# A searched order of steps for the third and the last attention of a four-layer transformer kernel

## What is computed

```python
x = x + tanh(g_xattn[2]) * L2_xattn(layernorm(x), ctx)   # 16 heads of 16, 154 context rows, softmax
x = x + tanh(g_ffn[2]) * L2_ffn(layernorm(x))            # 8 experts, two per token
x = x + tanh(g_xattn[3]) * L3_xattn(layernorm(x), ctx)   # 16 heads, queries and keys scaled to length 1,
                                                         # layernorm of (query + output) with gain and shift
x = x + tanh(g_ffn[3]) * L3_ffn(layernorm(x))            # 16 routed experts, two per token, and a shared one
```

## Time and profile before

| | us |
|---|---|
| median of three runs | 1379.36 |
| lowest and highest of them | 1375.1, 1379.63 |
| the profiled execution | 1367.15 |
| its span, first to last instruction | 1365.4 |
| PE busy in it | 1221.3 |
| DVE, ACT, POOL busy in it | 683.4, 473.6, 284.0 |
| third attention and its routing | 557 to 778 of the span |
| last attention and its routing | 942 to 1131 of the span |

### The profile page before, as it was taken

How to read it: one execution, slowest core, us unless ns; L and a number is a source line. 1 busy time by engine, 2 the same in 40 slices (tenths; PEclk the granted TensorE clock), 3 DMA queues, 4 the chain that set the end, 5 groups by cost and what they waited for, 6 DMA issues and landing times.

```text
span 1365.4 us, 19716 instructions
## 1 busy us (share of the span) xinstructions
PE 1221.3 (89%) x7073; PEld 765.9 (56%) x7073; DVE 683.4 (50%) x1969; ACT 473.6 (35%) x903; POOL 284.0 (21%) x372
## 2 busy tenths in 40 slices
PE   4999979999999765799999799993899988999997
PEld 2545444345667624445555599992455555666664
DVE  5565454577545485666566522224546771222114
ACT  1154524443232173124443133331665312223220
POOL 4200020020200102121024422222322361222220
PEclk9799989999999987679999699997999998999998
DMA  9994010001000100000002777755000224444415
GB/s 249 273 273 141 1 58 1 0 1 62 1 1 1 35 0 0 2 20 2 1 31 94 243 218 210 215 167 167 1 1 5 99 83 132 148 154 154 145 61 185
DMA packets 106494, 124.06 MB, mean 91 GB/s; under 512 B 15554, under 2 KB 90942, under 8 KB 106398
## 3 DMA queue, kind: packets, MB, share of 16 engines
q1 hardware_dynamic: 99406, 103.92, 26.3%
q0 software_dynamic: 6992, 18.88, 3.7%
HBM read 73.92 MB, written 48.86 MB: 90 GB/s over the span
## 4 chain that ended last, share of the span: by engine, by line
PE 81%; DVE 7%; issue 4%; ACT 3%; POOL 3%; DMA 1%; SPq 1%; DVEq 0%; POOLq 0%; ACTq 0%
PE bank L1225 9%; PE bank L848 6%; PE bank L1259 5%; PE bank L774 5%; PE bank L1301 5%; PE bank L1268 5%; PE bank L868 5%; PE bank L909 4%; PE bank L1059 3%; PE bank L912 3%; PE bank L757 3%; PE bank L715 2%; PE bank L1016 2%; PE bank L921 2%; POOL x_slots L1768 2%
## 5 line engine op out<-in xcount | busy, mean ns | idle before, releaser
L1225 PE MATMUL bank<-scratch 128*128 128x320 f32 (+3 forms) x480 | 151.2, 472 | 0.6 <-issue 0.6
L2098 DVE TENSOR_REDUCE scratch<-bank 128x2 f32<-128x308 f32 x256 | 103.9, 472 | 62.1 <-PE bank L848 61.7
L1372 ACT ACTIVATE scratch<-bank 128x512 f32<-128x512 f32 x192 | 99.2, 604 | 64.9 <-PE bank L875 48.1
L1225 PEld LDWEIGHTS bank<-scratch 128*128 128x128 f32 (+1 forms) x480 | 86.1, 183 | 60.2 <-issue 28.5
L2606 DVE TENSOR_TENSOR scratch<-scratch,bank 128x320 f32<-128x320 f32 (+3 forms) x60 | 31.4, 525 | 170.3 <-PE bank L1225 170.1
L1741 POOL TENSOR_SCALAR rstd<-mv 128x4 f32<-128x4 f32 x36 | 9.0, 249 | 475.5 <-DVE mv L1879 461.9
L848 PE MATMUL bank<-scratch 32*128 32x308 f32 x512 | 80.5, 512 | 3.8 <-DVE scratch L2098 1.7
L1259 PEld LDWEIGHTS bank<-scratch 128*128 128x128 f32 x624 | 77.3, 195 | 2.6 <-issue 0.7
L2589 DVE TENSOR_TENSOR scratch<-bank,weights 128x512 f32<-128x512 f32 x39 | 27.0, 692 | 102.8 <-PE bank L1259 102.8
L1863 POOL DMA_INDIRECT y_back<-scratch x48 | 45.2, 941 | 157.6 <-ACT scratch L1609 138.4
L1259 PE MATMUL bank<-scratch 128*128 128x128 f32 x624 | 77.6, 279 | 0.3 <-issue 0.3
(11 more groups left out here) (385 smaller groups left out, 2223.6 us busy)
## 6 DMA issues: line engine op xcount, KB each, us to landing
scratch<-in_L_ffn_W SPq DMA_DIRECT2D x47, 512.0 KB, 4.0
x_slots<-zeros SPq DMA_DIRECT2D x1, 17680.0 KB, 76.4
scratch<-y_back SPq DMA_DIRECT2D x16, 512.0 KB, 7.8
scratch<-in_L_ffn_w_gate SPq DMA_DIRECT2D x16, 352.0 KB, 3.1
scratch<-in_L_ffn_w_up SPq DMA_DIRECT2D x16, 352.0 KB, 3.8
x_slots<-zeros SPq DMA_DIRECT2D x1, 5200.0 KB, 94.2
scratch<-x_slots SPq DMA_DIRECT2D x39, 130.0 KB, 3.0
y_back<-zeros SPq DMA_DIRECT2D x1, 4352.0 KB, 39.9
```

The lines of the kernel that those rows point to most:

```text
L1225: last = pe.matmul(bk[0:fn, 0:n], w[s][:, k, m * P:m * P + fn], moving(k), start=k == 0, stop=k == DK - 1)
L1372: act.activation(v["PT"][:, n % 2, j, :], bk[:], ACT.Exp, scale=float(v["hd"]) ** -0.5).then_inc(RP.read, 1)
L2098: dve.tensor_reduce(v["mx"][:, TPC * c + t, r, 2 * m:2 * m + 2], bk[:, 0:2 * M].rearrange("p (e k) -> p e k", k=M), AX.X, ALU.max)\
```

## The change

The tables `FIRST`, `EACH` and `LAST` get a new order for the third attention (`2`) and the last one (`3`). The entries of the first attention (`0`) and the hand-written list of the second stay. Since a row falls away in the table, every later line number is lower by one. On DVE, one wait for the engine's own earlier writes is put ahead of `down` of the shared expert, because `res`, which writes the same rows of X, may now stand directly before it. The diff, cut to two lines of a table and the code:

```diff
             3: [
-                ("combine", 0), ("stats", 0), ("normal", 0), ("yT", 0), ("combine", 1), ("stats", 1), ("proj", 0),
-                ("normal", 1), ("unit", 0), ("turn", 0)]}
+                ("combine", 0), ("stats", 0), ("normal", 0), ("combine", 1), ("yT", 0), ("proj", 0), ("stats", 1),
+                ("unit", 0), ("turn", 0), ("normal", 1)]}
...
                 elif what == "down":
+                    st.wait()
                     expert_out(p, E3, c, lambda t: gate)
```

More of the change, by code:

```diff
@@ L633, in build @@
             2: [
-                ("stats", 3), ("scores", 0, 0), ("norm", -1, 2), ("av", -1, 3), ("normal", 2), ("max", 1, 0, 0),
-                ("rem", 0), ("next b2", -3), ("max", 1, 0, 1), ("next scatter", -3), ("next yT", -2), ("av", 0, 0),
-                ("max", 1, 1, 0), ("scores", 0, 1), ("max", 1, 1, 1), ("norm", -1, 3), ("yT", 2), ("next lg", -2),
-                ("max", 1, 2, 0), ("turn back", -1), ("max", 1, 2, 1), ("av", 0, 1), ("max", 1, 3, 0),
-                ("scores", 0, 2), ("max", 1, 3, 1), ("next top", -2), ("proj", 2), ("tail", -1), ("next gates", -2),
@@ L639, in build @@
[L639 to L647 removed]
+                ("normal", 2), ("scores", 0, 0), ("max", 1, 0, 1), ("next b2", -3), ("yT", 2), ("next yT", -2),
@@ new lines, in build @@
+                ("max", 1, 1, 0), ("rem", 0), ("max", 1, 1, 1), ("norm", -1, 2), ("norm", -1, 3), ("scores", 0, 1),
+                ("max", 1, 2, 0), ("proj", 2), ("next lg", -2), ("stats", 3), ("turn back", -1), ("max", 1, 2, 1),
+                ("av", 0, 0), ("max", 1, 3, 0), ("scores", 0, 2), ("max", 1, 3, 1), ("next top", -2), ("av", 0, 1),
+                ("max", 2, 0, 0), ("tail", -1), ("next scatter", -3), ("next gates", -2), ("next stats", -1),
+                ("scores", 0, 3), ("norm", 0, 0), ("negm", 1), ("norm", 0, 1), ("next normal", -1), ("av", 0, 2),
@@ new lines, in build @@
+                ("next G", -2), ("av", 0, 3), ("next pos", -2)],
+            3: [
+                ("turn back", -1), ("next res", -3), ("next yT", -2), ("scores", 0, 0), ("next lg", -2),
+                ("proj", 1), ("next top", -2), ("combine", 3), ("scores", 0, 1), ("unit", 1), ("tail", -1),
+                ("next pos", -3), ("av", 0, 0), ("scores", 0, 2), ("norm", 0, 0), ("av", 0, 1), ("post", -1),
+                ("next scatter", -3), ("next stats", -1), ("turn", 1), ("norm", 0, 1), ("scores", 0, 3),
+                ("av", 0, 2), ("stats", 3), ("av", 0, 3), ("rem", 1), ("norm", 0, 2), ("norm", 0, 3),
+                ("next normal", -1), ("yT", 2), ("normal", 3)]}
@@ L653, in build @@
             2: [
-                ("av", 3, 3), ("next yT", 2), ("norm", 3, 2), ("norm", 3, 3), ("next lg", 2), ("next top", 2),
-                ("turn back", 3), ("next scatter", 1), ("ahead keys", 0), ("next gates", 2), ("tail", 3),
-                ("next G", 2), ("next stats", 3), ("next pos", 2), ("next normal", 3), ("ahead values", 0, 0),
-                ("next scatter", 2), ("ahead values", 0, 1), ("next yT", 3), ("next lg", 3), ("next top", 3),
-                ("next pos", 3), ("next gates", 3), ("next b2", 2), ("ahead unit keys", 0), ("next b2", 1),
@@ L659, in build @@
[L659 to L668 removed]
+                ("next yT", 2), ("norm", 3, 2), ("norm", 3, 3), ("next lg", 2), ("next top", 2), ("turn back", 3),
@@ new lines, in build @@
+                ("next scatter", 1), ("ahead keys", 0), ("next gates", 2), ("tail", 3), ("next G", 2),
+                ("next stats", 3), ("next pos", 2), ("next normal", 3), ("ahead values", 0, 0), ("next scatter", 2),
+                ("ahead values", 0, 1), ("next yT", 3), ("next lg", 3), ("next top", 3), ("next pos", 3),
+                ("next gates", 3), ("next b2", 2), ("ahead unit keys", 0), ("next b2", 1), ("next G", 3),
+                ("next b2", 3), ("ahead keys turned", 0), ("next scatter", 3)],
```

30 lines of the change are left out of this document (10 added, 20 removed).

## The result

| | before | after |
|---|---|---|
| median of the runs compared | 1377.23 us (1369.45 to 1379.63, 4 runs) | 1395.68 us (1392.62 to 1396.45, 4 runs) |
| profiled execution: time, span | 1367.15, 1365.4 us | 1392.62, 1390.9 us |
| mean granted clock | 0.935 | 0.919 |
| two attentions in the trace: third | 220.5 us | 229.6 us |
| last, with the routing up to the first expert's transposes | 188.7 us | 205.5 us |

The changed kernel is slower: ratio 1.014, 95% interval 1.009 to 1.019. The forecast was 1372.3 us, range 1363 to 1383. (The third attention is measured from its first transposes to the first product of the routed experts, the last one from its first transposes to the first expert's transposes, both on PE.

A forecast was written before the change was run, and what follows sets the result against it. PE, with 81% of the chain, was taken to bound the kernel (DVE and POOL the routing); -5.1 - 0.5 - 0.5 - 1.0 = -7.1 us from the 1379.36 us median gave 1372.3 us, range 1363 to 1383.

The forecast's parts named there:

- The last attention's body: Last attention, chunks 1 to 3: long work behind scores covers ACT's exponentials, 1.7 us won a chunk, -5.1 us.
- The opening: Last attention's opening: unit 0 -2.1, av 0 0 +2.8, fourth scores -1.2; together -0.5 us, bounds -3.3 and +1.6.
- The routing: Behind the last attention: DVE and POOL bound, the new order changes little; -0.5 us, bounds -1.5 and +2.
- The third attention: Third attention: 0.5 us from the projection's clock, 0.5 us between its chunks; -1.0 us, bounds -5 and +3.
- stretched places: Last attention: PE steps drawn long while waiting for a bank; 3.5 us a chunk before, 1.8 us left after.
- Rival 3: Waits only change place, a stretch taken from scores turns up elsewhere: -1 us, 1378.4 us; chance 0.13.
- no scores over 2 us: Sign of being right: no scores longer than 2 us in the last attention's chunks 1 to 3, except behind av.
- PEclk under 0.95: Sign of being wrong: windows of chunks 1 to 3 of the last attention with PE's clock below 0.95.
- both structural terms: Last attention's opening: unit 0's wait 2.1 us shorter, and 2.8 us lost waiting at av 0 0.
- rival 1: Short transpose rows bring four more clock falls in two attentions, 1.6 us each: -0.7 us, 1378.7 us; chance 0.15.
- Rival 2: POOL's scatter set behind post 2 delays next normal 2 and the last sets: +3.4 or +10.0 us; chance 0.14.
- the 6.9 us that did not raise the clock: Third attention's opening: keys and two transposed chunks ran 6.9 us without raising the clock, so only 0.5 us was taken.

The follow-up runs named there:

- after_again: The changed kernel run again, unchanged: 1370.57 us, 1.0031 of the kernel before.
- before_again: The kernel before, unchanged, as a control: 1365.30 us, 1.000 of the kernel before.
- last_only: The kernel before with only the last attention's tables of the change and the wait in "down": 1368.12 us, 1.0018 of the kernel before.
- first_new: The kernel before with only the last attention's opening list FIRST[3] of the change: 1368.94 us, 1.0016 of the kernel before.
- proj_late: The changed kernel with proj 1 and all later projections behind scores 0 1 in the last attention: 1375.14 us, 1.0064 of the kernel before.
- before_fill3: The kernel before with 28 unread identity transposes ahead of the third attention's first transposes: 1359.0 us, 0.9950 of the kernel before.
- scatter_early: The changed kernel with POOL's scatter sets back ahead of the av's and of post in both tables: 1384.63 us, 1.0136 of the kernel before.
- third_only: The kernel before with only the third attention's tables of the change: 1369.65 us, 1.0035 of the kernel before.
- mix: The kernel before with the third attention's tables and the last attention's opening list FIRST[3] of the change: 1371.28 us, 1.0032 of the kernel before.
- before_pad: The kernel before with 128 more already-satisfied waits on PE ahead of the third attention: 1369.75 us, 1.0039 of the kernel before.
- before_filled: The kernel before with unread transposes: 28 ahead of the third attention, 60 ahead of the last, 24 ahead of its unit 0: 1376.02 us, 0.9990.

## Why the prediction was wrong

The forecast was -7.1 us; where completions come in time the change measured +4.7 us (after_again's median), and on the chip of the first comparison +18.5 us. Two steps failed: the count of waits that remain in the last attention's body, and its opening, where waits were priced at a clock that was taken as given. Late completions had no term at all and are most of the first comparison's loss. In the traces of after_again and before_again the terms come out at about +0.9 us for the body (forecast -5.1), +4.6 us for the opening (-0.5), +0.5 us for the routing (-0.5) and -2.8 us for the third attention (-1.0). In last_only, with less half clock, they are about -0.8 us for the body and +2.0 us for the opening.

**The last attention's body, -5.1 us: wrong, and the step is the count of places that a new order frees.** I had priced 3.5 us of stretched places a chunk and left 1.8. In last_only, with no late completion and the clock at 1.00, chunk 1 still has them:

```profile
990.37 1.93 PE L867 MATMUL bank<-scratch 32*128 32x512 f32 x8
...
1002.45 1.97 PE L867 MATMUL bank<-scratch 32*128 32x512 f32 x8
...
1008.25 1.49 PE L867 MATMUL bank<-scratch 32*128 32x512 f32 x8
1010.21 1.06 PE L908 MATMUL bank<-scratch 128*32 128x512 f32 x8 [0.47 <-ACT scratch L1371]
...
1013.78 1.90 PE L889 MATMUL bank<-scratch 32*32 32x512 f32 x32
```

Against 1.14 us for a scores step and 1.23 us for `rem` that is 0.79 + 0.83 + 0.35 + 0.47 + 0.67 = 3.1 us where I had left 1.8. The first scores, which I had at 0.3, stand behind `turn back` and cost 0.8; the fourth, which I had at nothing, cost 0.35 and 0.47 for the `av` behind it. Chunk 2 gives the plainest test. It has the same 216 PE records in both orders, and there are traces of both with the clock at 1.00 throughout, here first_new (the body of before) and last_only (the new one), each from scores 2 0 to scores 3 0:

```profile
1016.70:1047.50 30.80, 30.16 (x217) 16.99 (x216) 18.18 (x77) 18.39 (x40) 6.18 (x7) 1.00 0.01 1
```

```profile
1020.00:1051.40 31.40, 29.73 (x217) 16.66 (x216) 20.61 (x77) 18.14 (x40) 6.18 (x7) 1.00 0.01 1
```

The chunk that was to win 1.7 us takes 0.6 us more. Over the whole stage PE is busy 164.1 us in last_only and 163.2 to 163.5 us in the traces with the tables of before. Rival 3 (waits only change place) is what happened in the body. The sign "no scores over 2 us" came true and was too coarse to tell anything; the sign of being wrong that did show is a PEclk under 0.95, 0.92 in chunk 3 of the changed kernel.

**The opening, -0.5 us: both structural terms right, the sum wrong.** The unit's wait fell by 2.1 us and `av 0 0` waits 2.7 to 2.8 us, within 0.1 us of the forecast. But a wait that shrinks is not yet time won, and I priced both at a clock that I took as given. In the first 50 us of the last attention the clock is at 0.50 for 12.4 us before (before_again) and 23.5 us after (after_again). Scores 1 0 come at 51.8 us for 42.7, of which some 4.5 us are work moved ahead (an estimate from the lengths of `rem`, one `av`, one `norm` step and `turn back` at full clock, 1.23 + 1.86 + 0.53 + 0.90 us): +4.6 us. In last_only, with the same instructions in this attention, the clock is at half for 16.3 us and scores 1 0 come at 49.2 us: +2.0 us. So the order alone does not set this price. first_new shows it for one term alone, 2.1 us won and 4.6 paid, 2.1 at `yT 1` and 2.5 with the clock. proj_late shows that the 2.8 us were no price either: taken away, nothing came back.

**The clock that falls in mid-chunk (rival 1): the price right, the cause not shown.** In after_again the clock falls 3.5 us behind the start of scores 2 0 and 4.6 us behind that of scores 3 0; chunk 2 takes 33.1 us with such a fall and 31.4 us in last_only without: 1.7 us for the 1.6 priced. That is one fall more in the last attention's chunks than before had, and one more in the third (705.6); the rival had four more and the forecast none. That the rows of transposes ahead of the scores bring the clock down is not shown: the same instructions ran with and without the fall, and so did the chunk of before (32.5 us with it in before_again, 30.8 us without it in first_new). By the Trainium skill (TensorE: Matmul & The Clock Gate, Part 4: PE-mode transpose) a transpose doesn't count as PE being busy. In the experiments here the fillers are transposes and nothing else, and in before_fill3 they held the clock at 1.00 where it fell at 553.0 in before_again. The measurement decides: transposes alone can keep the clock, so that rule does not explain the falls.

**The routing, -0.5 us: right within its bounds.** From `turn back 3` on it takes 53.7 us in after_again for 53.2 in before_again. In the first comparison it took 60.2 us, with the half clock and the late slots left by the late completions.

**Rival 2 (POOL, slower): wrong way round.** The set behind `post 2` was to hold the last sets up. scatter_early puts it back ahead and loses some 13 us. I had followed POOL's queue to `next normal 2` and not asked what `post 2` itself, and with it `norm` on DVE, would wait for.

**The third attention, -1.0 us, bounds -5 and +3: held by its bounds.** The traces give -2.9 us when the clock rises 3 us behind the first transposes (third_only) and +3.6 us when it rises 16 us behind them (mix); before's order gives 220 us in all six traces. The rows of third_only and mix:

```profile
555.80:559.00 3.20, 3.16 (x11) 2.36 (x12) 2.92 (x4) 1.19 (x2) 2.90 (x6) 0.51 0.01 3
559.00:572.60 13.60, 12.27 (x48) 5.94 (x48) 7.61 (x22) 1.37 (x2) 0.76 (x3) 1.00 0.00 1
```

```profile
555.70:571.50 15.80, 15.79 (x30) 6.99 (x31) 6.53 (x15) 1.88 (x3) 3.63 (x9) 0.50 0.01 2
```

Same instructions, same start to 0.1 us. That most executions are of the second kind would explain the 4 us by which third_only is slower than before; the traces (four short, three long) do not show it. (One reading was off: the 6.9 us that did not raise the clock held the keys and one turned chunk, not two. Nothing in the sum changes.)

**What no term held: late completions.** They make the result 1.4% instead of 0.3%, and lie in the third attention's chunk 3 and the last one's chunk 3 and routing. What they come from stays open. They came on one chip of the five groups, with scatter packets under way, in kernels of either order, and on that chip before took 13 us more too; I take the first comparison's chip as another such, or the same, since both medians agree with it to 1.3 us, but no trace of the kernel before was taken there with its late times. Packets of the instruction queue are excluded as the sole cause by third_only and before_pad; as a part of the cause on such a chip they are not. Not tried: the changed order without any scatter beside `rem` and `av`.

## What to carry to other kernels

An order that shortens waits by two microseconds is worth nothing if the engine's clock falls in the same place: read the granted clock of the stretch in more than one execution, and try the cheapest remedy first, here 28 transposes that nobody reads in a wait of 7 us. They were worth 6 us where a new order of two attentions was worth none, though on one chip only, and put into two other waits they did nothing. A stretched step behind a ring of banks is work owed by the reader of the banks; here moving steps on PE only moved the stretch. Less work on ACT or more banks might remove it; neither was tried. And before an instruction is moved past others on a queue, follow what waits for those: the scatter set was harmless behind the root and cost some 13 us ahead of it.

## What was new about the hardware

- On one chip, completions came up to 7.7 us late while the packets of 8 indirect DMAs ran (one issued every 1.27 us); on the others the same two programs, before and changed, had none over a microsecond. It is not PE's alone: in before_filled DVE waits up to 0.54 us for its own last result in the scatter stretch (packets 1062.5 to 1071.9), which in before_again it does not.

```profile
1069.45 0.57 DVE L2423 TENSOR_TENSOR scratch<-scratch 128x16 bf16<-128x16 bf16 x3 [0.37 <-DVE scratch L2423]
...
1070.88 0.18 DVE L2433 RECIPROCAL scratch<-scratch 128x4 f32<-128x4 f32 x1 [0.54 <-DVE scratch L2431]
```

- The clock's rise after a pause depends on more than the program: 3.2 and 15.8 us behind the same instruction in two kernels with the same third attention and the same code ahead of it, and 6.5 us of that attention's time.
- Transposes of the identity alone can keep the clock at 1.00: 28 ahead of the third attention did in four of five traces. In before_filled the 60 ahead of the last attention ran at once, ended 10.61 us before the first transposes that are needed, and did not hold it. Nor did the 24 ahead of `unit 0`, which ended 5.13 us early: the clock then fell at 961.5, 15.4 us behind the attention's first transposes for 12.4 us in before_again, and lay over the first scores.
